# A Mamba-2 block with experts on one core: decay differences from four bf16 pieces, and the first tap of B and C on GpSimd

## The reference

```python
zxbcdt = u @ in_proj_w.T
dt = softplus(zxbcdt[..., -NHEADS:] + dt_bias);  A = -exp(A_log)
xBC = silu(causal_conv(xBC, conv_w, conv_b))     # 4 taps; x has 256 channels, B and C 64 each
step:  h = h * exp(dt_t * A) + dt_t * x_t B_t;   y_t = h C_t
y = (y + D * x) * silu(z), normed                # once forward, once on the reversed tokens
x = x + ga * (y_fw + y_bw) @ out_proj_w.T
x = x + gb * expert_ffn(layernorm(x))            # each token goes to 1 of 8 experts
```

## Time and profile before

| | us |
|---|---|
| median of 3 runs (423.61 to 426.65) | 424.61 |
| the profiled execution's own time | 423.88 |
| its span, first to last instruction | 422.2 |
| PE / DVE / ACT / POOL busy | 381.2 / 341.9 / 299.6 / 321.2 |
| chunk loop, about | 36 to 317 |

### The profile page before, as it was taken

The page is one execution under the profiler, slowest core; times in us unless marked ns, Lnnn a source line. Parts: engine busy times, 40 slices in busy tenths (PEclk is TensorE's granted clock), DMA queues, the critical chain, the costliest instruction groups (busy, mean ns, idle before and its releaser), DMA issues. The chain is left out here.

```text
span 422.2 us, 10384 instructions
## 1 busy us (share of the span) xinstructions
PE 381.2 (90%) x3004; PEld 344.8 (82%) x3004; DVE 341.9 (81%) x1031; ACT 299.6 (71%) x866; POOL 321.2 (76%) x486
## 2 busy tenths in 40 slices
PE   8889989997998899699999899889998998999990
PEld 7757878897888798587889788779998887989990
DVE  6687789998879998989779998789688756768880
ACT  3776789797799988678677788898766665444430
POOL 4754894799995989679989889999947777765541
PEclk9999999999999999999999999999999999999996
DMA  8999999999940000001010110003921176888720
GB/s 228 330 334 335 334 336 331 334 334 330 325 127 2 1 2 2 0 2 50 2 53 2 50 51 3 2 0 110 379 68 39 54 216 177 264 253 234 223 78 0
DMA packets 54950, 63.27 MB, mean 150 GB/s; under 512 B 4604, under 2 KB 47996, under 8 KB 54768
## 3 DMA queue, kind: packets, MB, share of 16 engines
q1 hardware_dynamic: 50528, 55.76, 43.9%
q0 software_dynamic: 2784, 6.37, 4.1%
q10 hardware_dynamic: 1584, 0.50, 0.5%
HBM read 20.97 MB, written 42.09 MB: 149 GB/s over the span
## 5 line engine op out<-in xcount | busy, mean ns | idle before, releaser
L721 POOL TENSOR_TENSOR accb<-accb,prod 128x512 f32<-128x512 f32 x48 | 61.3, 1277 | 23.4 <-ACT accb L1144 19.4
L2036 DVE SCALAR_TENSOR_TENSOR bank<-raw,cw,bank 128x512 f32<-128x512 f32 x96 | 72.1, 751 | 2.2 <-ACT bank L1154 0.9
L754 POOL TENSOR_SCALAR lseg<-strict,av 128x128 f32<-128x128 f32 x128 | 47.8, 387 | 6.4 <-DVE av L1995 4.4
L1577 PE MATMUL bank<-skip,cx 128*128 128x128 f32 x256 | 41.2, 284 | 7.7 <-DVE st L2084 7.3
L1813 PE MATMUL bank<-raw 128*128 x312 | 43.5, 283 | 0.9 <-DVE raw L2459 0.9
L1193 ACT ACTIVATE xt<-bank,dtv 128x128 f32<-128x128 f32 x128 | 39.5, 362 | 5.2 <-PE bank L1556 4.9
L1577 PEld LDWEIGHTS bank<-skip,cx 128*128 128x128 f32 x256 | 33.6, 191 | 10.7 <-DVE st L2084 9.8
L955 POOL DMA_INDIRECT routed_rows<-rows,rowat x32 | 33.5, 1045 | 10.8 <-issue 9.1
L1051 POOL DMA_INDIRECT out_dram<-raw x26 | 25.7, 988 | 20.0 <-DVE raw L2485 13.3
L1813 PEld LDWEIGHTS bank<-raw 128*128 128x128 f32 x312 | 38.0, 192 | 1.7 <-issue 1.0
L1593 PE MATMUL bank<-xt,ms 128*128 128x128 f32 x256 | 39.0, 275 | 0.0
(11 more groups left out here) (294 smaller groups left out, 1134.8 us busy)
## 6 DMA issues: line engine op xcount, KB each, us to landing
routed_rows<-padrow SPq DMA_DIRECT2D x32, 1040.0 KB, 12.5
zs<-routed_rows SPq DMA_DIRECT2D x39, 130.0 KB, 3.3
xs<-in_w_dram SPq DMA_DIRECT2D x16, 258.0 KB, 3.6
hT<-in_w_dram SPq DMA_DIRECT2D x15, 258.0 KB
zs<-in_w_dram SPq DMA_DIRECT2D x8, 258.0 KB, 3.7
raw<-in_w_dram SPq DMA_DIRECT2D x1, 2048.0 KB, 10.0
xs<-in_u_dram SPq DMA_DIRECT2D x3, 512.0 KB, 8.2
routed_rows<-padrow SPq DMA_DIRECT2D x9, 130.0 KB, 3.2
```

The source lines that it names most:

```text
L721: pool.tensor_tensor(accb[:, :], accb[:, :], prod[:, :], ALU.add).then_inc(s_tapb, 1)
L754: last = pool.tensor_scalar(lseg[:, Q % LA, h, :], strict[:, d, :], av[:, b, col(d, h, t)], 1.0, ALU.mult, ALU.mult)
L1577: last = pe.matmul(bank[4 + Q % 2][:, h * HD:(h + 1) * HD], cx[:, S % 2, h, c0:c0 + P], skip[:, d * NH + h, :], start=(h == 0), stop=False ...
L2036: dve.scalar_tensor_tensor(out=acc(S, g)[:, :], in0=raw[:, g, c0:c0 + BLK], scalar=cw[:, d, g, k:k + 1], in1=acc(S, g)[:, :], op0=ALU.mult ...
```

## The change

The difference of the running sums of a between two tokens is no longer made by PE from a scaled triangle; the running sums themselves are computed once per batch (`cumulate`), cut into four bf16 pieces on DVE (`round_decays`, `cut_pieces`), transposed (`turn_pieces`) and kept by ACT (`keep_pieces`) as `pc` and, per head, `pch`. In each chunk two bf16 matmuls of 256 columns (one with a broadcast column as weights, one with a broadcast column as the moving side) add +cum(i) and -cum(j) to the mask. The start decay is now also an exponent: `pick`·`pc` lies beside it in the bank, `decays` takes exp of 384 columns instead of 256, and `cs` reads it from `es` in SBUF. `decay_rows` is gone. The first tap of B and C moves from ACT (`tap0_bc`) to POOL, ahead of tap k = 2.

```diff
@@ side_order
                 if (s, j) == (6, 1):
                     yield ("pfx", nxt)
+                    yield ("cum", nxt)
                 if (s, j) == (6, 3):
-                    yield ("erow", nxt)
+                    yield ("crow", nxt)
@@ taps_bc (POOL)
+                if k == HALO - 1:
+                    if S >= 1:
+                        hold(pool, s_bc, S)
+                    pool.tensor_scalar(accb[:, :], raw[:, NH, at_raw(b, blk):at_raw(b, blk) + BLK],
+                                       cw[:, d, NH, KC - 1:KC], cb[:, d, NH:NG], ALU.mult, ALU.add).then_inc(s_tap0b, 1)
@@ POOL
-            def decay_rows(Q):
...
-                if Q + LA < NCH:
-                    decay_rows(Q + LA)
@@ ACT
-            def start_rows_out(b):
+            def keep_pieces(b):
...
+                act.activation(pc[:, b, :, :], turned, ACT.Copy)
+                for h in range(NH):
+                    last = act.activation(pch[:, b, :, h, :], turned, ACT.Copy, scale=halves[:, h:h + 1])
+                last.then_inc(free(u), 1)
-            def tap0_bc(S):
...
-                act.activation(es[:, Q % 2, :, :], bank[2 + Q % 2][:, 0:DI].rearrange("p (h i) -> p h i", h=NH),
+                act.activation(es[:, Q % 2, :, :], bank[2 + Q % 2][:, 0:DI + P].rearrange("p (h i) -> p h i", h=NH + 1),
                                ACT.Exp).then_inc(s_e, 1)
@@ PE
                 for d in range(2):
-                    for k, m in enumerate((incl[:, d, :], strict[:, d, :])):
-                        pe.matmul(side(u)[:, k * NQ + d * W:k * NQ + (d + 1) * W], m, av[:, b, d * W:(d + 1) * W],
-                                  start=True, stop=True)
+                    pe.matmul(side(u)[:, d * W:(d + 1) * W], strict[:, d, :], av[:, b, d * W:(d + 1) * W],
+                              start=True, stop=True)
+            def cumulate(b):
...
+                pe.wait_ge(s_hilo, b + 1)
+                for d in range(2):
+                    last = pe.matmul(side(u)[:, d * 2 * W:(d + 1) * 2 * W], incl[:, d, :],
+                                     hilo[:, d].rearrange("p k c -> p (k c)"), start=True, stop=True)
@@ prepare
-                pe.matmul(sg[:, DI + P:DI + 2 * P], pick[:, t, :], eparts[:, b, d, :], start=True, stop=True)
+                pe.matmul(sg[:, DI:DI + P], pick[:, t, :], pc[:, b, d, :], start=True, stop=True)
                 pe.matmul(sg[:, 0:DI], identb[:, :], negm[:, d, :, :].rearrange("p h i -> p (h i)"),
                           start=True, stop=False, skip_group_check=True)
-                pe.wait_ge(s_L, Q + 1)
-                for h in range(NH):
-                    last = pe.matmul(sg[:, h * P:(h + 1) * P], lseg[:, Q % LA, h, :], incl[:, d, :],
-                                     start=False, stop=True, skip_group_check=True)
+                pe.matmul(sg[:, 0:DI], onet[:, t:t + 1].broadcast_to([P, P]),
+                          pch[:, b, d, :, :].rearrange("p h i -> p (h i)"), start=False, stop=False, skip_group_check=True)
+                last = pe.matmul(sg[:, 0:DI], pc[:, b, d, :],
+                                 minus[:, :].rearrange("p (h t) -> p h t", h=NH)[:, :, t].unsqueeze(2).broadcast_to([P, NH, P]),
+                                 start=False, stop=True, skip_group_check=True)
@@ PE, order
             sums(0)
+            cumulate(0)
             project(1, 0)
-            start_rows(0)
+            turn_pieces(0)
...
                     if (s, j) == (6, 1):
                         sums(nxt)
+                        cumulate(nxt)
@@ DVE
+            def round_decays(b):
...
+                cut(dve.tensor_scalar(some, decay, FLOOR, None, ALU.max))
+                cut(dve.tensor_scalar(hilo[:, :, 0, :], some, GRID, GRID, ALU.add, ALU.subtract))
+                dve.tensor_tensor(hilo[:, :, 1, :], some, hilo[:, :, 0, :], ALU.subtract).then_inc(s_hilo, 1)
+            def cut_pieces(b):
...
+                dve.tensor_copy(cumd[:, :, :, :].rearrange("p d k c -> p (d k c)"), side(u)[:, 0:4 * W]).then_inc(free(u), 1)
+                wait_free(dve, u)
+                cut(dve.tensor_copy(cpart[:, :, 0, :], cumd[:, :, 0, :]))
+                cut(dve.tensor_tensor(r[1], cumd[:, :, 0, :], cpart[:, :, 0, :], ALU.subtract))
+                cut(dve.tensor_copy(cpart[:, :, 1, :], r[1]))
+                cut(dve.tensor_tensor(r[2], r[1], cpart[:, :, 1, :], ALU.subtract))
+                cut(dve.tensor_tensor(r[3], cumd[:, :, 1, :], r[2], ALU.add))
+                cut(dve.tensor_copy(cpart[:, :, 2, :], r[3]))
+                dve.tensor_tensor(cpart[:, :, 3, :], r[3], cpart[:, :, 2, :], ALU.subtract).then_inc(s_cpart, 1)
-                dve.tensor_tensor(cs[:, Q % 2, :], cc[:, (Q // BT) % 2, c0:c0 + P], sg[:, DI + P:DI + 2 * P],
+                dve.tensor_tensor(cs[:, Q % 2, :], cc[:, (Q // BT) % 2, c0:c0 + P], es[:, Q % 2, NH, :],
                                   ALU.mult).then_inc(s_m, 1)
@@ DVE, order of the prologue (at (5,3) and (6,2) in the loop)
             softplus_end(0)
+            round_decays(0)
             taps_x(0, 1)
+            cut_pieces(0)
             gate_bc(0)
-            decay_copies(0)
             gate_x(0, 1)
-            cut_starts(0)
-            cut_rest(0)
```

More of the change, by code:

```diff
@@ L33 @@
 MASKED = -30000.0
+FLOOR = -110.0
+GRID = 24576.0
+NP = 4
 NTOK = B * L
@@ L166 @@
 WARM_SUMS, WARM_STARTS = 6, 3
-OTHER = (1, 2, 2, 3, 5, 4, 4)
+OTHER = (1, 2, 2, 3, 5, 4, 0, 4)
 for _bank, _key in enumerate((("o", B * NBLK - 1, 0), ("o", B * NBLK - 1, 1),
-                              ("xT", 1), ("xT", 2), ("xT", 3), ("pfx", 0), ("erow", 0))):
+                              ("xT", 1), ("xT", 2), ("xT", 3), ("pfx", 0), ("cum", 0), ("crow", 0))):
     USE[_key] = LATE + _bank
@@ L664, in _ @@
                                     pattern=[[-1, P]], channel_multiplier=1))
-            link(pool.tensor_tensor(ident3[:, :], ident[0:3 * W, 0:W], ident[0:3 * W, W:2 * W], ALU.add))
-            link(pool.tensor_tensor(ident3[:, :], ident3[:, :], ident[0:3 * W, 2 * W:3 * W], ALU.add))
+            link(pool.tensor_tensor(ident4[:, :], ident[:, 0:W], ident[:, W:2 * W], ALU.add))
+            for c in range(2, NP):
+                link(pool.tensor_tensor(ident4[:, :], ident4[:, :], ident[:, c * W:(c + 1) * W], ALU.add))
             hold(pool, s_fill0, 3)
@@ L974, in cut_b2 @@
                 hold(pool, s_b2, 10)
-            for Q in range(LA):
-                decay_rows(Q)
             raw_bc_there(1)
@@ L1282, in _ @@
             keep_b(0)
-            start_rows_out(0)
+            keep_pieces(0)
             c_over_b(0)
@@ L1357, in _ @@
                 if nxt is not None and (s, j) == (7, 0):
[L1358 removed]
+                    keep_pieces(nxt)
                 if g is not None and j == 0:
@@ new lines, in cut @@
+            def cut(ins):
+                ncut[0] += 1
+                ins.then_inc(s_cut, 1)
+                dve.wait_ge(s_cut, ncut[0])
+            def round_decays(b):
+                decay = av[:, b, :].rearrange("p (d c) -> p d c", d=2)
+                some = rest[:, 0, :].rearrange("p (d c) -> p d c", d=2)
+                dve.wait_ge(s_a, b + 1)
+                cut(dve.tensor_scalar(some, decay, FLOOR, None, ALU.max))
+                cut(dve.tensor_scalar(hilo[:, :, 0, :], some, GRID, GRID, ALU.add, ALU.subtract))
+                dve.tensor_tensor(hilo[:, :, 1, :], some, hilo[:, :, 0, :], ALU.subtract).then_inc(s_hilo, 1)
@@ new lines, in cut_pieces @@
+            def cut_pieces(b):
+                u = USE["cum", b]
+                r = [rest[:, k, :].rearrange("p (d c) -> p d c", d=2) for k in range(4)]
+                wait_full(dve, u)
+                dve.tensor_copy(cumd[:, :, :, :].rearrange("p d k c -> p (d k c)"), side(u)[:, 0:4 * W]).then_inc(free(u), 1)
[7 more added lines that the diff above has]
+                dve.tensor_tensor(cpart[:, :, 3, :], r[3], cpart[:, :, 2, :], ALU.subtract).then_inc(s_cpart, 1)
@@ L2260, in _ @@
             softplus_one(0)
+            dve.tensor_scalar(minus[:, :], ident4[:, :], -1.0, None, ALU.mult)
+            dve.tensor_tensor(onet[:, :], ident4[:, 0:TPB], ident4[:, TPB:2 * TPB], ALU.add)
+            dve.tensor_reduce(halves[:, :], ident4[:, :].rearrange("p (h t) -> p h t", h=NH), AX_X, ALU.add)
             for k in range(2 * NH):
@@ L2333, in _ @@
                     carry(Q)
-                if nxt is not None and (s, j) == (7, 0):
-                    cut_starts(nxt)
-                if nxt is not None and (s, j) == (7, 1):
-                    cut_rest(nxt)
                 conv_b(S, j)
@@ L2381, in _ @@
                         softplus_end(nxt)
+                        round_decays(nxt)
                     if (s, j) == (6, 2):
-                        decay_copies(nxt)
+                        cut_pieces(nxt)
             ne = [0]
```

117 lines of the change are left out of this document (40 added, 77 removed).

## The result

The changed kernel takes 431.5 us (median of 4 runs, 430.97 to 431.83), the kernel before, timed beside it, 424.23 us (4 runs, 423.61 to 426.65). The ratio is 1.0159, with a 95% interval of 1.0117 to 1.0202: slower by about 7.3 us, where 418.5 with a range of 410 to 428 was forecast.

The account below looks back on a forecast made before the run. The loop was taken to be paced by PE and DVE in turn, POOL's load covered. Terms -10.8 + 1.8 - 3.0 - 2.0 + 5.4 - 1.0 + 1.5 + 2.0 = -6.1 gave 418.5 us, range 410 to 428.

Parts of the forecast that it names:

- PE in each chunk, -10.8: Decay matmuls: two bf16 matmuls replace the float32 pair, saving 0.23 us in 47 of 64 chunks, -10.8 us.
- In the other 47 it does: PE's saving of 0.23 us buys time in the 47 chunks where DVE is not full: -10.8 us.
- the port: Rival: POOL's unbroken taps behind gate_bc stretch every cs within them, 16.6 us instead of 5.4; 429.7 us, chance 0.10.
- DVE absorbs it: Rival: shorter PE just waits longer for the new state, a third of 10.8 arrives; 425.7 us, chance 0.22.
- ACT, +1.8 and -3.0: Wider es lengthens DVE's wait in 17 places, +1.8 us; first taps leaving ACT recover half of 6.1 us of waits, -3.0.
- POOL, -2.0: POOL loses decay_rows and gains 16 first taps; of ACT's 3.3 us of waits for POOL, 2.0 us go.
- `cs`, +5.4: In the chunks, cs reads SBUF twice and is hit 16 times by POOL's adds, at most 10.6 us: +5.4 us.
- Prologue, +1.5: Batch 0's table work ahead of the first chunk makes that chunk later by 1.5 us.
- Tables -1.0: Batch 1's tables: 3 + 8 small DVE instructions replace some ten wider ones where DVE is full, -1.0 us.
- the bank +2.0: At y_turn of (6,2) PE waits for DVE's copy of cum out of its bank: nothing to 2.8, taken as +2.0 us.

Follow-up runs that it names:

- the version with two exp: Changed kernel with table work reordered and the start exponent's exp done separately in PSUM, where cs reads it: 0.9944, second run 0.9980 of the kernel before.
- e2: Changed kernel with cs reading the start exponent from PSUM, its exp not used: ratio 1.0012 to the kernel before.
- the one with the new order: Changed kernel with its table work split and moved, nothing computed otherwise: ratio 1.0018 to the kernel before.
- the one with warm matmuls: Changed kernel with float32 matmuls of unused results in three places where the granted clock had fallen: ratio 1.0173 to the kernel before.

## Why the prediction was wrong, step by step

**PE in each chunk, -10.8: the price was right, the effect was not.** The saving of 0.22 us a chunk is there (0.11 per new matmul). The failed sentence is "In the other 47 it does": a PE that is busy 94% of the time was taken for a PE that sets the pace. One decay matmul fewer in the kernel before gave 0.9984, 0.7 us for 14.1; in the 32 chunks where its clock stayed whole, 1.0 us for 7.0. In the changed kernel PE's waits for the new state of DVE rose from 7.3 us in 10 places to

```profile
PE bank L1572 <- DVE st L2084: 15.7, 25, 2.5
```

The chain through a chunk runs over PE, ACT, DVE and back; PE's shorter part ends in a longer wait for `st`. What the change is worth without the port show `cs` from PSUM (98.3 and 132.8 us in the stretches of 24 and 32 chunks, against 101.4 and 135.1) and the version with two exp, in its second run (98.7 and 133.0). That is 5.4 and 4.8 us less, where PE, ACT, POOL and `es` together were to bring 14.0 (-10.8 + 1.8 - 3.0 - 2.0), most of it there. A third or so arrived, as the rival "DVE absorbs it" had supposed for PE's part.

**ACT, +1.8 and -3.0.** `es` came out at 494 ns against my 392 + 110. DVE's wait for it rose only from 9.9 us in 17 places to

```profile
DVE ms L2069 <- ACT es L1195: 10.7, 18, 1.8
```

and moving the tap back showed no change, so of the 3.0 nothing was seen.

**POOL, -2.0.** ACT's waits for POOL fell from 3.3 us to 1.4, and no time can be seen to have come of it. 37 us of POOL's load in the loop went, and were covered before, as I had read.

**`cs`, +5.4: right mechanism, and a size that two errors made right.** I forecast 16 hits behind POOL's adds, at most 10.6 us, half of it on the path. There were 23 long ones, 8.2 us, and 5 to 6 us came of it (`e2`). Seven of the 23 ended behind an add of the taps, two behind an add of the second layernorm, the other 14 behind or within a POOL instruction with one tensor input, which my sum did not have. So hits behind adds were little more than half as many as forecast, others made up for them, and a larger share reached the path (0.65 to 0.75 instead of 0.5). That the term came out near its size is luck. In DVE's order of time in the changed kernel:

```profile
33.05 0.68 DVE L2056 SCALAR_TENSOR_TENSOR cc<-bc,accb 128x512 f32<-128x512 f32 x1
...
39.91 1.17 DVE L2274 TENSOR_TENSOR gb_sum<-gbias 128x8 f32<-128x8 f32 x1
41.01 3.53 DVE L2277 TENSOR_SCALAR won<-yzb,nw 128x128 f32<-128x128 f32 x4
...
44.79 0.91 DVE L2071 TENSOR_TENSOR cs<-cc,es 128x128 f32<-128x128 f32 x1
...
102.25 1.29 DVE L2071 TENSOR_TENSOR cs<-cc,es 128x128 f32<-128x128 f32 x1
...
119.46 0.28 DVE L2071 TENSOR_TENSOR cs<-cc,es 128x128 f32<-128x128 f32 x1
...
129.81 0.51 DVE L2071 TENSOR_TENSOR cs<-cc,es 128x128 f32<-128x128 f32 x1
```

and in POOL's:

```profile
39.80 1.26 POOL L733 TENSOR_TENSOR accb<-accb,prod 128x512 f32<-128x512 f32 x1
...
42.27 2.19 POOL L964 TENSOR_TENSOR rows<-rows,b2p 96x1024 f32<-96x1024 f32 x1
...
102.12 1.26 POOL L733 TENSOR_TENSOR accb<-accb,prod 128x512 f32<-128x512 f32 x1
...
117.58 2.91 POOL L767 TENSOR_TENSOR rn<-rt,mhalf 128x16 f32<-128x16 f32 x1
...
129.49 0.69 POOL L728 TENSOR_SCALAR prod<-raw,cw 128x512 f32<-128x512 f32 x1
```

At 102.25 `cs` ends with an add, as expected. At 129.81 it ends behind `prod`, a POOL instruction with one tensor in SBUF: 130.32 after 130.18. This is the wider rule of the Trainium skill (SBUF — State Buffer, "Who interferes with whom"), that a GpSimd instruction reading SBUF shuts out a DVE instruction with two SBUF inputs. I had cited it and summed without it; for 20 of the 23 long ones, which end 0.14 to 0.15 us behind a POOL instruction, the trace agrees with the page. It does not for all of POOL's instructions: at 119.46 `cs` lies wholly within POOL's `rn` (117.58 to 120.49 by its record, small tensors of 128x16) and takes its usual 0.28 us, and three of the 23 (at 97.70, 223.76 and 300.94) end 0.2 us ahead of the POOL instruction that they overlap. Where page and trace differ, the trace decides: not every overlap is a hit.

**Prologue, +1.5, measured +5.1.** `gate_bc` starts at 33.05, as forecast. On ACT:

```profile
35.41 0.63 ACT L1171 ACTIVATE cc<-cc 64x512 f32<-64x512 f32 x1
35.94 1.05 ACT L1098 ACTIVATE raw<-bank 128x512 f32<-128x512 f32 x2
...
40.02 0.60 ACT L1183 ACTIVATE xt<-bank,dtv 128x128 f32<-128x128 f32 x2
```

`c_over_b` is at 35.41, forecast was 35.5. Two things were missing. Behind `c_over_b` on ACT stands `keep_raw(1, 0)`, and `project_z` waits for its bank: it starts at 36.57 and takes 2.07 us at half clock, where in the kernel before it was

```profile
34.39 1.13 PE L1537 MATMUL bank<-wz,hT 128*128 128x256 f32 x4 [0.32 <-ACT raw L1102]
```

So the first `tokens_major` comes 2.4 us later (40.02 against 37.60), not 1.5; and ACT's `zt`, on which DVE's row of instructions ahead of the first `mix` waits, comes 3.1 us later (`zs` starts at 39.31, at 36.18 before). And POOL, free of `decay_rows`, now runs its adds and `cut_b2` over DVE's `gb_sum` and `won` (preparations made once) and its first `cs`. In the kernel before the first two were

```profile
36.79 0.16 DVE L2272 TENSOR_TENSOR gb_sum<-gbias 128x8 f32<-128x8 f32 x1
36.87 2.39 DVE L2275 TENSOR_SCALAR won<-yzb,nw 128x128 f32<-128x128 f32 x4
```

The stretching is (1.17 - 0.16) + (3.53 - 2.39) + (0.91 - 0.27) = 2.8 us. It meets PE's stream at `ms`·`xt` of chunk 0, which started at 40.78 before without a wait. In the changed kernel, in the one with the new order and in the one with warm matmuls, in this order:

```profile
45.75 0.71 PE L1588 MATMUL bank<-xt,ms 128*128 128x128 f32 x4 [0.95 <-DVE cs L2071]
```

```profile
43.79 0.72 PE L1590 MATMUL bank<-xt,ms 128*128 128x128 f32 x4 [2.20 <-DVE cs L2077]
```

```profile
45.24 0.71 PE L1588 MATMUL bank<-xt,ms 128*128 128x128 f32 x4 [1.78 <-DVE cs L2075]
```

So in the changed kernel about 4 of the 5.1 us had come down PE's own stream (the late `project_z` and the half clock until 42.8), and DVE's lateness, 3.1 + 2.8 us less the slack of 1 us that it had before, adds the last one. Taking one of the two away leaves most of the loss: a whole clock there brought chunk 0 only 0.5 us forward, and the new order only 2.0, since PE then waits for DVE's `cs`. That `gb_sum`, `won` and `cs` are stretched by POOL is read from the overlap; no run took POOL's work away from there.

**Tables -1.0 and the bank +2.0, measured together +4.7.** The mechanism at (6,2) is the predicted one: PE waits 2.63 us for the copy of `cum` (forecast: up to 2.8). The rest was not in the sum: `round_decays` lengthens DVE's unbroken block ahead of `mix` at (5,3), PE waits 2.47 us there for the new state (1.64 before), and at both waits a stretch at half clock begins, against my reading of a clock of 1.00 throughout. By the pairs above a fall costs 1.4 to 1.5 us here, so two of them are most of what the forecast missed. The new order removes the 2.63 us wait, has one fall instead of two, and takes 40.5 instead of 44.5 us.

**The account.** The spans differ by +7.8 us where the sum had -6.1. The miss of 13.9 is made up, rounding aside, of 6.9 in the 56 plain chunks (-1.7 for -8.6), 3.6 in the prologue, 3.7 in chunks 24 to 31 (+4.7 for +1.0), and -0.2 behind. The 56 chunks' own miss is the absorbed saving (5.4 instead of 14.0, by `e2`); the port cost 3.1 to 3.7 us there (-1.7 + 4.8, -1.7 + 5.4), less than the 5.4 that I had for the whole loop. The rivals were each priced with everything else as in the forecast; two of them, absorbed and port, came together. My reading is that what shortened PE made DVE's chain the last to arrive while the same change stretched DVE; the runs show both parts, not that one made the other dearer.

What stays open: how the 1.4% of the new order and the 1.5% of `cs` divide, since each alone brings the kernel back to the one before while both together, with the second exp, reach only 0.9944 and 0.9980, with a prologue 2 to 3 us later than before; and how much of any ratio here is the clock, which fell in other places in almost every kernel.

## What to carry to other kernels

Before crediting a saving to the busiest engine, ask what it waits for as soon as it is faster; where four engines are each busy for 80 to 94%, a cut of 14 to 18 us on one alone was worth a tenth of its size or less here, and a stretch of one instruction in each chunk more than half. Look at the granted clock of every variant before reading its time: a PE with less to do waits longer, and its clock may fall. When an operand moves from PSUM to SBUF, count the DVE instructions that then read SBUF twice against POOL's instructions with one tensor input as well as against its adds, and count again wherever the change moves POOL's queue in time. When a table is computed once a batch, find the engine order around it: 11 small instructions cost about 3 us themselves, but in chunks 24 to 31 what stood behind them cost 4 us, and an order that lets PE's bank go first gave these back.

## What was unexpected of the hardware

- A POOL `tensor_scalar` of 512 columns with one tensor input holds up DVE's two-SBUF multiplication as its adds do: 0.51 us instead of 0.28 at 129.81, up to 1.29 behind an add.
- It works the other way round too: POOL's first tap took 0.76 us at its shortest and 1.71 us at 184.66, while DVE ran four instructions with SBUF inputs:

```profile
184.66 1.71 POOL L724 TENSOR_SCALAR accb<-raw,cw,cb 128x512 f32<-128x512 f32 x1 [2.73 <-ACT raw L1098]
```

```profile
184.22 1.66 DVE L2112 SCALAR_TENSOR_TENSOR yzf<-yzb,rn,yzf 128x256 f32<-128x256 f32 x4
```

- But a POOL instruction on small tensors (`rn`, 128x16, 2.91 us) did not hold up a `cs` that ran wholly within it.
- The fall of the granted clock at a PE idle of about 2 us came in one execution of a kernel and not in another on a second chip; where it came, seven chunks took 1.5 us more.
- Less work for PE can lose clock: with 14 us of matmuls left out, three PE waits of 1.9 to 2.8 us were each followed by half clock, 17 us in all, where the kernel before had none.
